# Diagonal blocks of the first eight row tiles: two GpSimd operations per group of four, in place of one vector operation per tile

## The reference, cut to what matters

```python
# x: (8, 2048, 128) f32, adj: (2048, 2048) f32, W: (128, 128) f32
h = jnp.maximum(_layernorm(x, axis=-1), 0.0)
HW = jnp.einsum('bnf,fo->bno', h, W)
A_norm = jax.nn.relu((adj + adj.T) * 0.5)
D = jnp.sum(A_norm, axis=1)
D_safe = jnp.where(D > 0, D, 1.0)
d_inv_sqrt = jnp.where(D > 0, D_safe ** (-0.5), 0.0)
DAD = d_inv_sqrt[:, None] * A_norm * d_inv_sqrt[None, :]
L_norm = jnp.eye(N) - DAD
out = jax.nn.relu(jnp.einsum('nm,bmo->bno', L_norm, HW))
return x + out
```

## Time and profile before

| | us |
|---|---|
| median of 3 runs (401.29 to 401.61) | 401.59 |
| the profiled execution, its own time | 401.33 |
| its span in the profile | 399.5 |
| PE busy | 375.5 |
| DVE busy | 311.1 |
| ACT busy | 192.5 |
| POOL busy | 117.0 |

### The profile page before, as it was taken

One profiled execution on the slowest core, in us unless ns is written; L12 is line 12 of the kernel. 1 busy time (PEld: TensorE's weight loads), 2 busy tenths in 40 slices (PEclk: granted clock), 3 DMA queues, 4 the chain that ended last, 5 costly groups with the idle time before them and its releaser, 6 DMA issues.

```text
span 399.5 us, 6166 instructions
## 1 busy us (share of the span) xinstructions
PE 375.5 (94%) x2144; PEld 201.3 (50%) x2144; DVE 311.1 (78%) x606; ACT 192.5 (48%) x416; POOL 117.0 (29%) x253
## 2 busy tenths in 40 slices
PE   3568899989999999999999999999999999999995
PEld 3568854434444444545454445444544544454454
DVE  2868799788799887999879679967965796679246
ACT  1576876889976777867854133212211121113001
POOL 0496006678678245453511120400000000000000
PEclk9998999999999999999999999999999999999999
DMA  8999997012325431342254049921130122012203
GB/s 256 387 388 386 384 279 218 26 53 64 97 80 191 151 106 54 112 153 80 80 184 132 26 122 345 298 79 54 53 106 2 53 77 83 2 53 79 80 27 107
DMA packets 69567, 55.00 MB, mean 138 GB/s; under 512 B 2848, under 2 KB 58272, under 8 KB 69536
## 3 DMA queue, kind: packets, MB, share of 16 engines
q1 hardware_dynamic: 69536, 54.60, 42.8%
HBM read 39.91 MB, written 14.68 MB: 137 GB/s over the span
## 4 chain that ended last, share of the span: by engine, by line
PE 76%; DVE 14%; ACT 3%; issue 3%; DMA 2%; SPq 1%; DVEq 0%; ACTq 0%
PE ps L1256 11%; PE ps L1258 10%; PE ps L1257 10%; PE ps L1246 10%; PE ps L1240 10%; PE ps L1241 10%; PE ps L1154 4%; DVE S L846 3%; DMA S<-in_adj_dram 2%; DVE stats L803 2%; DVE S L819 2%; PE ps L1191 2%; PE ps L1292 2%; PE ps L1294 2%; PE ps L1293 2%
## 5 line engine op out<-in xcount | busy, mean ns | idle before, releaser
L1240 PE MATMUL ps<-S,hbuf 128*128 128x512 f16 x240 | 91.0, 379 | 1.4 <-ACT S L695 1.4
L1241 PE MATMUL ps<-S,hbuf 128*128 128x512 f16 x240 | 91.0, 379 | 0.0
L1246 PE MATMUL ps<-S,hbuf 128*128 128x512 f16 x256 | 76.2, 379 | 0.1
L1256 PE MATMUL ps<-S,hbuf 128*128 128x512 f16 x152 | 57.6, 379 | 0.0
L1257 PE MATMUL ps<-S,hbuf 128*128 128x512 f16 x152 | 57.6, 379 | 0.0
L1258 PE MATMUL ps<-S,hbuf 128*128 128x512 f16 x152 | 57.6, 379 | 0.0
L735 ACT ACTIVATE g<-ps 128x512 f16<-128x512 f32 x31 | 18.3, 595 | 68.0 <-DVE ps L926 32.0
L674 ACT ACTIVATE ps<-hbuf,lnt 128x128 f32<-128x128 f32 x112 | 44.9, 449 | 4.9 <-DVE hbuf L809 4.9
L846 DVE SCALAR_TENSOR_TENSOR S<-S,dneg 128x512 f16<-128x512 f32 x54 | 40.1, 753 | 5.6 <-ACT S L695 5.4
L1246 PEld LDWEIGHTS ps<-S,hbuf 128*128 128x128 f16 x256 | 25.0, 98 | 30.6 <-DVE S L846 1.1
L695 ACT ACTIVATE S<-S,dneg 128x512 f16<-128x512 f32 x54 | 37.5, 716 | 5.9 <-DVE S L846 4.2
(11 more groups left out here) (143 smaller groups left out, 693.8 us busy)
## 6 DMA issues: line engine op xcount, KB each, us to landing
S<-in_adj_dram SPq DMA_DIRECT2D x15, 1024.0 KB, 14.5
hbuf<-in_x_dram SPq DMA_DIRECT2D x64, 128.0 KB, 3.1
sums<-in_x_dram SPq DMA_DIRECT2D x32, 256.0 KB, 2.9
out_dram<-sums SPq DMA_DIRECT2D x31, 256.0 KB, 2.3
t_forms<-work SPq DMA_DIRECT2D x24, 256.0 KB, 3.1
S<-t_forms SPq DMA_DIRECT2D x5, 1024.0 KB, 9.6
S<-in_adj_dram SPq DMA_DIRECT2D x2, 512.0 KB, 13.4
S<-t_forms SPq DMA_DIRECT2D x1, 768.0 KB, 9.7
```

Source lines behind the costliest of these rows:

```text
L1240: nc.tensor.matmul(acc, hbuf[:, u, 0, at:at + P], l_hi(t), start=(i == 0), stop=False)
L1241: nc.tensor.matmul(acc, hbuf[:, u, 1, at:at + P], l_hi(t), start=False, stop=False)
L1246: last = nc.tensor.matmul(acc, hbuf[:, u, 0, at:at + P], l_lo(t), start=False, stop=(i == T - 1))
L1256: nc.tensor.matmul(acc, a_hi, b_hi, start=starts, stop=False)
```

## The change

The eight diagonals of tiles 0 to 7 leave DVE's list. POOL makes those of one group of four tiles by two operations: a product of the identity and `dminus`, both broadcast to 128x512, into the idle `dsv[:, 0]`, and a sum of that with the four diagonal blocks of S, which are read and written with a stride. Group 0 stands behind POOL's early layer norm and ahead of the loop over slots, group 1 at slot 10 of that loop, ahead of the `normalise` of the same slot. ACT's waits count groups for tiles 0 to 7; the eight late diagonals, still on DVE, have a semaphore of their own.

```diff
+DIAG_AT = 10
...
+            def take_diags(g):
+
+                if g == 0:
+                    pool.wait_ge(d_ready, 1)
+                made = dsv[:, 0, :].rearrange("p (i f) -> p i f", i=GRP)
+                if g:
+
+                    pool.wait_ge(s_diag, g)
+                nc.gpsimd.tensor_tensor(made, ident[:].unsqueeze(1).to_broadcast([P, GRP, P]),
+                                        dminus[:, GRP * g:GRP * (g + 1)].unsqueeze(2).to_broadcast([P, GRP, P]),
+                                        ALU.mult).then_inc(diag_made, 1)
+                pool.wait_ge(diag_made, g + 1)
+                first = GRP * g * (N + P)
+                rows = S[:].rearrange("p t n -> p (t n)")
+                blocks = rows[:, first:first + GRP * (N + P)].rearrange("p (i n) -> p i n", n=N + P)[:, :, 0:P]
+                nc.gpsimd.tensor_tensor(blocks, blocks, made, ALU.add).then_inc(s_diag, 1)
...
+            take_diags(0)
             for tau in range(SLOTS):
+                if tau == DIAG_AT:
+                    take_diags(1)
                 if tau in DSV_AT:
...
-                if mt // GRP == g:
-                    act.wait_ge(s_diag, mt + 1)
+                if mt // GRP == g < 2:
+                    act.wait_ge(s_diag, g + 1)
+                elif mt // GRP == g:
+                    act.wait_ge(s_diag_late, mt - HALF + 1)
...
-                nc.vector.scalar_tensor_tensor(d, ident[:], dminus[:, mt:mt + 1], d, ALU.mult, ALU.add).then_inc(s_diag, 1)
+                nc.vector.scalar_tensor_tensor(d, ident[:], dminus[:, mt:mt + 1], d, ALU.mult, ALU.add).then_inc(s_diag_late, 1)
...
-                        if t >= LEAD - GRP:
-                            take_diag(t - (LEAD - GRP))
...
-                if tau < GRP:
-                    take_diag(GRP + tau)
...
-                                dve.wait_ge(s_diag, HALF + i + 1)
+                                dve.wait_ge(s_diag_late, i + 1)
```

More of the change, by code:

```diff
@@ L321, in gnn_layer @@
         h_lo_ready = sem("h_lo_ready")
+        diag_made = sem("diag_made")
         s_diag = sem("s_diag")
+        s_diag_late = sem("s_diag_late")
         l_hi_ready = sem("l_hi_ready")
```

## The result

The changed kernel takes **402.56 us** (median of 8 runs, 402.43 to 403.07) against 401.36 us before (8 runs beside it, 401.29 to 401.61): a ratio of 1.0031, with a 95% interval of 1.0022 to 1.0041. It is slower by 1.2 us, 0.3%. The time lies in the range that was given, 400.6 to 402.9; the likeliest case was "within 0.2%", and it came out just beyond, in the case that had a chance of 0.30.

The account below looks back on a forecast made before the run. PE is busy 94%; the ACT/DVE split delays its first sweep, so speeding the split gives at most 1.97 us. Terms -1.55 + 1.45 + 0.7 = +0.6 us give 401.9; forecast 402.0 us, range 400.6 to 402.9.

Parts of the forecast that it names:

- The gain of 1.55 us: First sweep, up to ACT's first L674: without the eight diagonals on DVE it starts 1.55 us earlier.
- the ring of ACT and DVE: Split without diagonals: high half waits for low half two pieces back, low for its own high; 1.55 us per two pieces.
- The share of the chain, 2.1 us: Chain of waits, 50 to 85 us: the eight diagonals (DVE L830) take 5.9%, 2.1 us; not all comes back.
- The cost at group 0, 1.45 us: From 59.72 us: POOL's two operations delay DVE's low half 0 by 0.38 and low half 1 by 1.07 us.
- PE pushed back by 0.7 us at no cost: PE's second slot: pushed back some 0.7 us, inside the 1.41 us that PE loses later at 89.01.
- the signs of error: Listed as wrong: L846 at 0.75 throughout beside POOL, PE's start moved from 60.23, or new PE gaps behind 104.
- the signs of being right: Included an early L846 of about 1.8 us, L674 at 73.3, L846 lengthened 0.4 near 78.2, PE wait 1.3-2.0 near 89.
- The cost at group 1, 0.7 us: Slot 10, near 78 us: POOL's two operations delay low half 15 by 0.44 and low half 16 by 0.25 us.
- the slower rival: POOL's first group 1 operation starts within 0.25 us before low half 15: net +1.0, 402.4 us; chance 0.3.
- POOL gives way at the start: Group 0: low half 1 precedes POOL's second operation, which costs 0.25, not 1.07; at best 400.4 us; chance 0.15.
- POOL holds DVE up to its own end: All four collisions: each costs 0.2 us more, 402.7 us; chance 0.05.
- The change does nothing: Both groups: gain and cost meet below 0.1 us, or missed slack takes the rest, 401.4 us; chance 0.1.

## Why the prediction was right or wrong

**The gain of 1.55 us** (eight diagonals off DVE, the ring of ACT and DVE): right, 1.58 us measured with neither engine making them, and 1.56 at the operation up to which it was walked. The share of the chain, 2.1 us, would have been a third too much.

**The cost at group 0, 1.45 us:** this is the term that failed; it measured 1.81 us in the change (low halves 0 and 1 end at 63.42 in place of 61.61). The step that failed is "low half 0 ends 0.56 after that, at 61.32, where it ended at 60.94 (+0.38)": it lets POOL's product run beside L835 (now L860) and dpos at no cost and meet low half 0 first. The sentence ahead of it, "Operations with an input in PSUM, and the statistics with one input, keep their durations", holds for what it names (the statistics keep their 0.86 us), but it says nothing of these two, whose one input is in SBUF, and I put them at nothing without a row for it. Both were held: by 0.88 and 1.07 us, less the 0.14 us for which low half 0 had been waiting for ACT. A hint was in the trace of before: L835 made its 256 columns in 0.35 us, as long as L830 takes for 128 in the earlier trace rows, where the rate of L846 and L830 gives 0.48. With 0.22 us of each operation for the start (0.35 less 128 columns of 0.38/384), L835 went, by this estimate, at about twice the rate. With the form that keeps a sum the same columns take 0.48 us and are not held. The Trainium skill (SBUF — State Buffer, section "SBUF: two separate sides") names this case beside the one with two SBUF inputs: an operation of VectorE in a 2-port mode contends as well. The trace, which shows durations and no modes, agrees, with 1.23 us against 0.48.

**That the size was nearly right all the same** is luck: 1.45 us was worked out from two operations that were not touched. It came out near because in these kernels the cost depends little on which operations are held: two low halves (1.9 us when GpSimd starts later), L860 and dpos (1.81 net), or dpos and the low halves (1.51 with the form that keeps a sum, 42.67 against 41.16).

**PE pushed back by 0.7 us at no cost:** right as to the end; GpSimd half a microsecond later gives PE its start back and nothing else. A late start of PE was listed among the signs of error, and it came, at 60.98. Of the signs of being right, the low half of 1.8 us among the first two did not come (the two together take 1.40), nor the wait near 89 us of 1.3 to 2.0 us (it is 0.89); ACT's first L674 stands at 73.68 and not 73.3, and the low half near 78.2 was lengthened by 0.71 and not 0.4. What I left out is that PE may lose clock behind such waits (twice in three profiled executions that have them). Of the change's eight runs three lie at 402.85 to 403.07 and five at 402.43 to 402.60; whether those three are such executions was not seen, since the profiled one kept the full clock.

**The cost at group 1, 0.7 us:** the mechanism right, the size 0.96 us. In the prediction's picture POOL's product starts 0.44 us ahead of low half 15; in the change it was 0.15 us (78.45 against 78.60), since POOL had gone from one normalise to the next without a gap (72.27 to 72.43) after its late start. That is the case of the slower rival, "the full price at 78 us", a start within the last 0.25 us ahead of low half 15. It had 0.9 and 0.25 us for it, where 0.71 and 0.25 came. With group 1 alone on GpSimd it was 0.44 us ahead and cost 0.66.

**The sum:** -1.58 + 1.81 + 0.96 = +1.19 us, and +1.21 on the path, +1.20 in the medians; the prediction had +0.6. The two terms missed by 0.36 and 0.26 us in the same direction, which carried the time across 0.2%. The slower rival had 402.4 us by too small a cost at group 0 and too large a one at group 1; that it lies nearest to the 402.56 measured is partly chance.

**The rivals.** "POOL gives way at the start" is out: with GpSimd held back so that its pair met the low halves, the sum went in between low halves 0 and 1, and the two took 3.30 us. "POOL holds DVE up to its own end" is out: low halves end 0.55 us after POOL's operation, L860, 0.35 us long, 0.15 us after it. "The change does nothing" is out too: the change is slower beyond the noise, and the runs that do one part of it show gain and cost apart.

## What to carry to other kernels

Moving small work from DVE to GpSimd is no saving when DVE is in the middle of operations with two SBUF inputs or of fast one-input ones: look at what DVE has in hand at that moment, not at whether GpSimd is idle, and reckon up to GpSimd's duration less 0.2 us for each large operation, less where DVE's operation starts later than GpSimd's (0.42 us at a start 0.44 us behind, 0.71 at 0.15). Where an engine waits for another in turn, look first for a slot in which it stands idle: here four operations put there by a change of order alone gave 0.5 us (400.98 against 401.49) that their move to another engine lost again. And price a removed operation by the ring that is left, not by its share of the chain.

## What the hardware showed that I had not expected

- An operation of sixteen elements per partition, 0.23 us alone, took 1.30 us beside a GpSimd operation of 1.26 us: that it reads so little did not save it.
- GpSimd's operation went first even where DVE's shows the earlier start in the profile, by 0.04 us at 59.65 and again at 60.26 with GpSimd's start held back.
- The same tensor_scalar takes 0.35 us alone and 1.23 beside GpSimd's product, but 0.48 us beside it in the form that also keeps a sum.
- After waits of PE of 1.17 (or 1.16) and 0.81 us near 61 and 63 us the granted clock fell to the 1.2 GHz level for some three microseconds in two of the profiled executions, and in the profiled one of the change, after waits of the same length (60.98 and 62.81), it stayed at full speed through this stretch. With group 1 in the idle slot the profiled run, which lost this way, took 402.81 us, 1.0 us more than the median of its program; that the other runs kept the clock was not seen.
